# Half of each expert's down product in fp32r parts, weight loads in halves, and an early first gather

## The reference

```python
x = x + _L0_xattn_ref(_layernorm(x), ctx_1024, ...)      # cross attention, 4096 keys a batch
x = x + _L0_attn_ref(_layernorm(x), ...)                 # 16 heads, window 64
x = x + _L0_ffn_ref(_layernorm(x), gate_w, wg, wu, wd)   # 8 experts, the best 2 for each token
# the experts:
logits = x_flat @ gate_w.T
top_v, top_i = jax.lax.top_k(logits, 2)
probs = jax.nn.softmax(top_v)
hidden = jax.nn.silu(x_flat @ wge.T) * (x_flat @ wue.T)  # 256 -> 1024, for each expert e
acc = acc + we[:, None] * (hidden @ wde.T)               # 1024 -> 256
```

## Time and profile before

| | us |
|---|---|
| median of 3 runs (lowest, highest) | 628.83 (628.47, 631.97) |
| the profiled execution, its own time | 628.76 |
| its span in the profile | 626.9 |
| busy PE, DVE, ACT, POOL | 604.3, 459.5, 336.0, 266.0 |

### The profile page before, as it was taken

How to read it: one execution, slowest core, us unless ns; L and a number is a source line. 1 busy time by engine, 2 the same in 40 slices (tenths; PEclk the granted TensorE clock), 3 DMA queues, 4 the chain that set the end, 5 groups by cost and what they waited for, 6 DMA issues and landing times.

```text
span 626.9 us, 10864 instructions
## 1 busy us (share of the span) xinstructions
PE 604.3 (96%) x4049; PEld 517.7 (83%) x4049; DVE 459.5 (73%) x812; ACT 336.0 (54%) x604; POOL 266.0 (42%) x321
## 2 busy tenths in 40 slices
PE   8999999899999999998999998999999999999995
PEld 7889988898889988996676776888888888888884
DVE  4877688866977698768898966876867667676851
ACT  4547523673257423562867672665564747565550
POOL 4317920684147531695454533134242433324222
PEclk9999999999999999999999989999999999999999
DMA  8988887899869836872000494899999999999642
GB/s 288 334 302 229 274 314 198 226 278 298 301 178 291 236 86 188 226 208 68 2 2 2 159 396 160 315 322 346 330 331 357 316 356 328 355 328 357 237 151 84
DMA packets 66147, 152.89 MB, mean 244 GB/s; under 512 B 7648, under 2 KB 47968, under 8 KB 55200
## 3 DMA queue, kind: packets, MB, share of 16 engines
q1 hardware_dynamic: 61728, 146.04, 69.8%
q0 software_dynamic: 4368, 6.16, 5.0%
HBM read 121.91 MB, written 31.59 MB: 245 GB/s over the span
## 4 chain that ended last, share of the span: by engine, by line
PE 76%; DVE 9%; POOL 6%; ACT 3%; issue 3%; DMA 2%; POOLq 0%; DVEq 0%; ACTq 0%
PE psum L1719 19%; PE psum L1326 14%; PE psum L1451 13%; PE psum L1736 12%; PE psum L1491 9%; POOL wide_low L610 4%; PE psum L1401 2%; DVE head_max L990 2%; DVE region_a L995 1%; POOL wide_high L608 1%; PE psum L1367 1%; PE psum L1331 1%; PE psum L1594 1%; PE psum L1534 1%; DMA region_w<-sums_by_token,tokens 1%
## 5 line engine op out<-in xcount | busy, mean ns | idle before, releaser
L704 ACT ACTIVATE wide_high<-region_a 128x1024 fp32r<-128x1024 f32 (+1 forms) x108 | 107.7, 998 | 95.4 <-PE psum L1719 95.4
L1156 DVE TENSOR_TENSOR wide_low<-region_a,wide_high 128x1024 fp32r<-128x1024 f32 x92 | 112.2, 1222 | 57.9 <-ACT wide_high L704 57.9
L610 POOL TENSOR_TENSOR wide_low<-region_a,wide_high 128x512 fp32r<-128x512 f32 x64 | 82.4, 1289 | 18.3 <-ACT wide_high L704 14.2
L1736 PE MATMUL psum<-region_a,region_w 128*128 128x256 f32 x368 | 83.3, 379 | 0.0
L1491 PE MATMUL psum<-turned_high,wide_low 128*128 128x256 f32 x256 | 79.7, 311 | 2.4 <-DVE turned_low L1067 1.6
L1719 PE MATMUL psum<-wide_low,turned_high 128*128 128x512 f32 x184 | 77.9, 424 | 0.2 <-DVE turned_high L1258 0.2
L1736 PEld LDWEIGHTS psum<-region_a,region_w 128*128 128x128 f32 x368 | 69.7, 190 | 10.2
L1719 PE MATMUL psum<-wide_high,turned_low 128*128 128x512 f32 x184 | 72.4, 393 | 0.0
L1491 PE MATMUL psum<-turned_high,wide_high 128*128 128x256 f32 x256 | 72.2, 282 | 0.0
L1491 PE MATMUL psum<-turned_low,wide_high 128*128 128x256 f32 x256 | 72.2, 282 | 0.0
L1719 PE MATMUL psum<-wide_high,turned_high 128*128 128x512 f32 x184 | 72.1, 392 | 0.0
(11 more groups left out here) (230 smaller groups left out, 1241.9 us busy)
## 6 DMA issues: line engine op xcount, KB each, us to landing
region_a<-turned_up SPq DMA_DIRECT2D x23, 2048.0 KB, 10.1
region_a<-turned_down SPq DMA_DIRECT2D x23, 1024.0 KB, 7.5
region_a<-ctx_dram SPq DMA_DIRECT2D x16, 1024.0 KB, 9.1
turned_up<-region_w SPq DMA_DIRECT2D x64, 256.0 KB, 4.0
region_w<-L_ffn_wg_dram SPq DMA_DIRECT2D x16, 512.0 KB, 6.1
region_w<-L_ffn_wu_dram SPq DMA_DIRECT2D x16, 512.0 KB, 6.2
region_w<-L_ffn_wd_dram SPq DMA_DIRECT2D x16, 512.0 KB, 5.8
turned_down<-region_w SPq DMA_DIRECT2D x32, 256.0 KB, 3.9
```

Source lines behind the costliest of these rows:

```text
L610: nc.gpsimd.tensor_tensor(val_lo[:, g % 4], ctx_sb[n][:, g * PAIR:(g + 1) * PAIR, :], val_hi[:, g % 4].bitcast(F32), ALU.subtract).then_in ...
L704: return nc.scalar.activation(dst, src, ACT.Copy)
L1156: nc.vector.tensor_tensor(w_lo[:, k % RING], group_of(k), w_hi[:, k % RING].bitcast(F32), ALU.subtract).then_inc(low_ready, 1)
L1736: last = nc.tensor.matmul(to[:, 0:D], hidT[n][:, ic * P:(ic + 1) * P], rows, start=ic == 0, stop=ic == IC - 1)
```

## The change

1. For tiles 0 to 21 (`WIDE` = 22) the second half of the down product (hidden columns 512 to 1023) is made of fp32r parts. ACT copies the second half of the down weights to `down_hi` at the start of the next tile, DVE subtracts to get `down_lo` (`low_down`), and ACT's second half of `hidT` goes to `hidT_hi`, from which DVE makes `hidT_lo` (`low_hidT`). Four plain products become twelve in fp32r. The parts of the weights take the SBUF space of `xnT`, and those of `hidT` the free half of the `turned` parts.
2. Each up load becomes two of 1 MB, wg's columns and wu's, with rows of 4 KB and a semaphore each; the first half waits only for the first two low parts of tile j - 3. Each down load becomes two of 512 KB with rows of 4 KB.
3. The spare gather reads rows of `turned_up` instead of `normed_rows`. It waits only for the weight stores, and stands on POOL ahead of the normalised rows. The waits for `rows_stored` and `zero_stored` stand ahead of the first gather on tokens.

```diff
+WIDE = SLOT_TILES - 1
...
-        xnT = sb("xnT", DC * TOK)[:, :].rearrange("p (c n) -> p c n", c=DC)
+        with nc.sbuf_tensor("xnT", [P, DC * TOK], F32) as until_routed:
+            xnT = until_routed[:, :].rearrange("p (c n) -> p c n", c=DC)
+        HALF = MAT // 2
+        down_hi, down_lo = [sb(name, HALF, F32R)[:, :] for name in ("down_high_part", "down_low_part")]
...
+        hidT_hi, hidT_lo = [t[:, 2 * DC * P:] for t in turned_parts]
...
+        def second_half(j):
+            return w_down[j % 2].rearrange("p (a k h x) -> p h a k x", a=QUADS, k=KPI, h=2)[:, 1]
+
+        def halved(parts):
+            return parts.rearrange("p (a k x) -> p a k x", a=QUADS, k=KPI)
...
             def load_up(j):
                 n = j % UPS
                 rows = expert_of(up_dram, j)
-                if j >= UPS:
-                    sp.wait_ge(low_ready, (j - UPS + 1) * 4)
-                sp.dma_start(w_up[n].rearrange("p (c n) -> p c n", c=DC), rows.rearrange("a (c p) n -> p (a c) n", p=P)).then_inc(up_loaded[n], 16)
+                to = w_up[n].rearrange("p (c n) -> p c n", c=DC)
+                held = rows.rearrange("a (c p) n -> p (a c) n", p=P)
+                for h in range(2):
+                    if j >= UPS:
+                        sp.wait_ge(low_ready, (j - UPS) * 4 + 2 * h + 2)
+                    part = slice(h * INNER, (h + 1) * INNER)
+                    sp.dma_start(to[:, :, part], held[:, :, part]).then_inc(up_loaded[n][h], 16)
...
             def load_down(j):
                 n = j % 2
                 rows = expert_of(down_dram, j)
                 if j >= 2:
                     sp.wait_ge(y_done, j - 1)
-                sp.dma_start(w_down[n], rows.rearrange("a p n -> p (a n)")).then_inc(down_loaded[n], 16)
+                held = rows.rearrange("a p n -> p (a n)")
+                for part in (slice(0, MAT // 2), slice(MAT // 2, MAT)):
+                    sp.dma_start(w_down[n][:, part], held[:, part]).then_inc(down_loaded[n], 16)
...
+            for n in range(2):
+                pool.wait_ge(w_stored[n], 16 * QUADS * E * NMAT // 2 + FIRST)
+            pool.indirect_dma_start(out=xg[AHEAD - 1], out_offset=None, in_=up_dram.rearrange("e d (a n) -> (e d a) n", n=D),
+                                    in_offset=bass.IndirectOffsetOnAxis(ap=spare_i[:, 0:1], axis=0)).then_inc(spare_gathered, 16)
             for s in range(2):
...
-            pool.wait_ge(rows_stored, 16 * DUOS)
-            pool.wait_ge(zero_stored, 32)
-            pool.wait_ge(w_turned, E * NMAT * STEPS)
-            pool.indirect_dma_start(out=xg[AHEAD - 1], out_offset=None, in_=x3_dram,
-                                    in_offset=bass.IndirectOffsetOnAxis(ap=spare_i[:, 0:1], axis=0)).then_inc(spare_gathered, 16)
             pool.wait_ge(rstd3_ready, len(LAST_ROWS))
             pool.wait_ge(behind_ready, 1)
             nc.gpsimd.tensor_tensor(behind[:, :], behind[:, :], rstd[:, :], ALU.mult).then_inc(behind_scaled, 1)
             pool.wait_ge(spare_gathered, 16)
+            pool.wait_ge(zero_stored, 32)
+            pool.wait_ge(rows_stored, 16 * DUOS)
             pool.wait_ge(tokens_ready, 1)
...
             def tile_step(j):
                 n = j % 2
-
+                if 0 < j <= WIDE:
+                    if j == 1:
+                        act.wait_ge(rows_stored, 16 * DUOS)
+                    else:
+                        act.wait_ge(y_done, j - 1)
+                    act.wait_ge(down_loaded[1 - n], 32 * ((j - 1) // 2 + 1))
+                    copy(halved(down_hi), second_half(j - 1)).then_inc(down_high, 1)
                 high(4 * j + 3)
                 if j > 0:
...
-                    act.wait_ge(up_loaded[(j + 1) % UPS], 16 * ((j + 1) // UPS + 1))
+                    act.wait_ge(up_loaded[(j + 1) % UPS][0], 16 * ((j + 1) // UPS + 1))
                     high(4 * j + 4)
                 if j > 0:
                     tile_hidT(j - 1, 1 - n)
                 if j + 1 < SLOT_TILES:
                     high(4 * j + 5)
+                    act.wait_ge(up_loaded[(j + 1) % UPS][1], 16 * ((j + 1) // UPS + 1))
                     high(4 * j + 6)
...
             def tile_hidT(j, n):
                 for half in range(2):
                     act.wait_ge(hid_turned, j * 2 + half + 1)
-                    copy(hidT[n][:, half * BANK:(half + 1) * BANK], bank[4 + half]).then_inc(hidT_ready, 1)
-
+                    to = hidT[n][:, half * BANK:(half + 1) * BANK]
+                    if half == 1 and j < WIDE:
+                        if j > 0:
+                            act.wait_ge(y_done, j)
+                        to = hidT_hi
+                    copy(to, bank[4 + half]).then_inc(hidT_ready, 1)
+
+            act.wait_ge(up_loaded[0][1], 16)
...
+            def low_down(j):
+                dve.wait_ge(down_high, j + 1)
+                nc.vector.tensor_tensor(halved(down_lo), second_half(j), halved(down_hi.bitcast(F32)), ALU.subtract).then_inc(down_low, 1)
+
+            def low_hidT(j):
+                dve.wait_ge(hidT_ready, j * 2 + 2)
+                nc.vector.tensor_tensor(hidT_lo, bank[5], hidT_hi.bitcast(F32), ALU.subtract).then_inc(hidT_low, 1)
+
             for j in range(SLOT_TILES):
                 n = j % 2
+                if 0 < j <= WIDE:
+                    low_down(j - 1)
...
                     tile_xgT(j + 1, 1 - n)
+                if 0 < j <= WIDE:
+                    low_hidT(j - 1)
...
+                    pe.wait_ge(hidT_low, j)
...
-                pe.wait_ge(down_loaded[n], 16 * (j // 2 + 1))
+                pe.wait_ge(down_loaded[n], 32 * (j // 2 + 1))
                 if 0 < j < SLOT_TILES - 1:
                     pe.wait_ge(y_ready, j)
                 for ic in part:
                     if ic % TPG == 0:
                         pe.wait_ge(hidT_ready, j * 2 + ic // TPG + 1)
                     rows = w_down[n].rearrange("p (a k q c r) -> p q k c a r", a=QUADS, k=KPI, q=QUADS, c=DC)[:, ic // KPI, ic % KPI]
-                    last = nc.tensor.matmul(to[:, 0:D], hidT[n][:, ic * P:(ic + 1) * P], rows,
-                                            start=ic == 0, stop=ic == IC - 1)
+                    cols = slice(ic * P, (ic + 1) * P)
+                    if ic < TPG or j >= WIDE:
+                        last = nc.tensor.matmul(to[:, 0:D], hidT[n][:, cols], rows, start=ic == 0, stop=ic == IC - 1)
+                    else:
+                        if ic == TPG:
+                            pe.wait_ge(down_low, j + 1)
+                            pe.wait_ge(hidT_low, j + 1)
+                        cols = slice((ic - TPG) * P, (ic - TPG + 1) * P)
+                        for m, (held, w) in enumerate(((hidT_hi, down_lo), (hidT_hi, down_hi), (hidT_lo, down_hi))):
+                            rows = w.rearrange("p (a k q c r) -> p q k c a r", a=QUADS, k=KPI, q=QUADS // 2, c=DC)[:, (ic - TPG) // KPI, ic % KPI]
+                            last = nc.tensor.matmul(to[:, 0:D], held[:, cols], rows, start=False, stop=ic == IC - 1 and m == 2)
```

5 lines of the change are left out of this document (3 added, 2 removed).

## The result

| | us | ratio to before, 95% interval |
|---|---|---|
| before, median of 20 | 629.77 | |
| changed, median of 20 | 632.09 | 1.0028 [1.0015, 1.0041] |
| changed, the profiled execution (span) | 633.22 (631.5) | |

The forecast was 621.8 and the range ended at 629.5. By the prediction's bound of 0.5% it is no change, though the interval lies wholly on the slower side. (The two medians alone have the ratio 1.0037.) Where 7 us were to be gained, 2.3 were lost, so some 9 us went somewhere else. One caution for all sums from the profiles: the profiled execution of the kernel before (628.76) was 1.0 us faster than its median, that of the changed kernel 1.1 us slower, so the spans differ by 4.6 us where the medians differ by 2.3.

The account below looks back on a forecast made before the run. PE was taken to bound the routed tiles, with DMA nearly full. From 628.76 us: down product -6.0, late scaling +0.65, gather -1.9, load stall +0.3, giving 621.8; range 619.5 to 629.5, the forecast's own 619.5 to 624.5.

Parts of the forecast that it names:

- The down product: Routed tiles: four plain products become 12 fp32r ones of 0.12 us, 0.285 us less a tile, period 9.77, -6.0 in all.
- rival (c): Down product: fp32r products run at 0.216 us with their strided view, +0.87 a tile, about 646 us; chance 0.07.
- New work on ACT and DVE: Routed tiles: ACT's copy costs nothing in idle time; DVE's two subtractions bring its busy time to 8.90 of 9.77 us.
- In the middle nobody waits for it soon: Routed tiles: the result's scaling, 1.0 us after the product's end instead of 0.39, costs nothing before the end.
- The end: After result 20: the chain runs over the late scaling of the result, +0.65 us.
- The moved gather: Entry of the routed stage: first gather on tokens issued at 381.3, landing 3.12 us later; gain 1.9, 2.0 at most.
- Loads: Routed stage: the DMA queue grows, a down load ends at 12.5 us against 11 allowed; stall 0.3 us in all.
- service times: DMA's time to serve a tile in the routed stage: 9.98 us, or 10.18 with 0.2 for the added packets.
- three transfers a tile: Routed stage: three transfers a tile fill the DMA engines' time without gaps, against a fixed 2 us for each.
- (a): Routed stage: DMA takes over and loads limit; 624.9 us, up to 627.5 with some gather loss; chance 0.17.
- (b): Routed stage loads: 4 KB rows serve worse than the bounds; at a service of 11.0, 635.1 us; chance 0.10.
- Rival (d): Routed stage: DVE's low part or the first gather lands late, only a part remains, 627 to 630 us; chance 0.08.

Follow-up runs that it names:

- e4: Changed kernel with each gather on tokens issued one tile earlier in POOL's order, ahead of the scatter it stood behind; 624.86 us, ratio 0.9915.
- e7: Changed kernel, gathers in their old place, odd tiles' scatters adding into a DRAM tensor of their own; 628.52 us, ratio 0.9967.
- e13: Changed kernel, gathers in their old place, without the one-element addition ahead of each scatter; 627.23 us, ratio 0.9948.
- e14: Changed kernel, gathers in their old place, odd scatters into a tensor of their own and no one-element addition; 623.33 us, ratio 0.9893.
- e3: Kernel before with only point 2, loads in halves with 4 KB rows and the earlier first half; 637.59 us, ratio 1.0103.
- e12: Changed kernel with whole loads: fp32r parts and moved spare gather, token gathers in their old place; 629.21 us, ratio 0.9968.
- e2: Kernel before with only point 3, the moved spare gather; 628.12 us, ratio 0.9960.

## Why the prediction was wrong

- **The down product: right.** 0.12 us a product in the strided view; unstalled tiles of 9.77; rival (c) did not come.
- **New work on ACT and DVE: right in size, and the failed step.** DVE was busy 182.44 of 200 us in e4, 8.91 a tile; forecast 8.90. The scaling of the result was put at 0.65 us later and it is. "In the middle nobody waits for it soon" is what failed. The order of POOL has scatter(j) behind it and gather(j + 4) behind that, whose rows PE needs 13 us after the product's end. The gather is issued late for reasons that the changed kernel brings together: a scatter that must wait for the landing of the one before it, while the period shrank to 9.77 and the landings grew from 7.3 to 9.0 us; an addition that a subtraction on DVE holds for up to 1.2 us; and, in tiles that follow no gap, y 0.6 us later. The first two are shown by e7, e13 and e14, the part of the halves by e3 and e12; the 0.6 us of y has no run of its own. In the kernel before, a gather had from its issue at 497.6 until PE's turn of it at 508.3, 10.7 us, for a landing of 8.1 on average and 9.2 at most (the nine gathers for which the view gives it): a slack of 1.5 to 2.6 us, and in no view a wait. The diff does not touch `gather_rows`; its slack was never worked out. Forecast for this: 0; measured: 9.8 us in the profiled execution, and 7.2 between the medians of the changed kernel and e4.
- **The end: right as far as it went.** 0.65 forecast, 1.38 measured: y was 0.7 late, and the addition's 1.0 us beside DVE was missed; the last scatter landed 0.4 sooner.
- **The moved gather: right in kind, 1.9 forecast, 0.7 to 0.8 seen.** The changed kernel's rows:

```profile
381.19 0.18 DVE L1277 TENSOR_TENSOR tokens<-spare_or_none,psum 128x23 int32<-128x23 f32 x1
...
382.17 1.05 POOL L663 DMA_INDIRECT region_w<-normed_rows,tokens  x1 [7.16 <-DVE tokens L1277]
...
385.84 0.44 PE L1370 MATMUL psum<-ident,region_w 128*128 128x128 f32 x2 [1.05 <-DMA region_w<-normed_rows,tokens]
```

  The tokens came 0.28 us later than before. From their end, 381.37, to the gather's issue lie 0.80 us, where 0.2 was assumed, and the rows were there 3.6 us after the issue, not 3.1. From the tokens' end to PE's turn of the rows it is 4.47 us instead of 5.46, a gain of 1.0; alone, with whole loads (e2), it is 1.7, and 2.3 in the medians.
- **Loads: no engine stalled for a weight load, as forecast within 0.3 us, but not for the reason given.** The halves of a down load landed in 5.4 us (median), not in times that grow along the stage to 12.5, and nobody waited for one:

```profile
region_a<-turned_down SPq DMA_DIRECT2D x46, 512.0 KB, 5.4
```

  No growth of a queue is seen. In e4, which kept up 9.77 us a tile with the same halves, the DMA share was 1.01 over 415 to 575, and up loads landed in 10.0 us (median) over 405 to 445 and 8.8 over 525 to 565. So the service times worked out from the DMA share, 9.98 and 10.18, were too high: a share near 1 was no proof that the engines had no more to give. The prediction's "three transfers a tile" is a misreading too; a tile had two weight loads, a gather and a scatter. Rivals (a) and (b) named the right resource for the wrong customer: what took longer were POOL's scatters, 9.0 us on average from issue to landing between 400 and 610 instead of 7.3. Their landing was put at nothing in the sum.
- **Rival (d), that only a part remains, was the nearest,** with 0.08 and no room for a result above 630; but neither of its conditions came (PE waited for no low part of DVE, and the first gather landed in 3.6 us), so it was near in the number alone.

The Trainium skill (SBUF — State Buffer, "Who interferes with whom") says that a VectorE instruction with two SBUF inputs contends with a GpSimd instruction that reads SBUF, and that the one issued second waits for the whole of the first. The rows agree: the addition issued at 504.65 ends at 505.85, with the subtraction of 504.57 to 505.80, and takes 0.19 where DVE is free. By that rule 1.0 us at the end (1.20 less 0.19) could have been in the sum. The same section has it that making descriptors is not held by such an instruction (marked there as inferred); here the issue of a scatter, which reads its row numbers from SBUF, took 2.63 us (at 506.01) when one was already running, and 1.59 when none was or when it began later (499.02), so for indirect transfers the measurement decides against it.

## What to carry to other kernels

When an edit delays an engine's output or shortens the period, follow every queue in which the consumer's instruction stands, to the next thing behind it that a fast engine needs, and work out its slack in both kernels: a slack of 2 us shows in no view until it is gone. Transfers that must come in time (gathers) belong ahead of those that only have to be done some time (scatters); that order cost nothing here and was worth 7 us. And a change of several parts should be read by its parts: the fp32r parts cost time until the order on POOL was mended and gained 4 us then, the moved gather gained in either order, and the loads in halves cost time in both (2.9 us in the changed kernel, 2.0 with early gathers).

## What the hardware showed beside this

- A one-element addition on GpSimd took 0.19 us with VectorE free and up to 1.26 us beside a two-input subtraction of 1024 columns on VectorE; the issue of an indirect scatter took 1.59 us, and 2.63 where such a subtraction was already running.
- With 1 MB of load issued 1.2 us behind it, a gather of 128 rows of 1 KB landed after 7.3 us instead of 3.1. Going first was no protection here.
- An indirect scatter with addition of the same size took 4.6 us on quiet queues (the end of the program) and 9.0 us on average in the stage of the changed kernel, with a spread to 11.6 us.
- The DMA engines showed a busy share of 1.01 over 160 us in e4 and still moved a tile's weights every 9.77 us; a tile of 10.06 us in the kernel before has the same share of 1.01.
